# Context transposed by a DMA instead of TensorE in a two-layer gated attention and expert kernel

## The reference, cut to what matters

```python
x = x + tanh(g_xattn[0]) * decayed_sum(layernorm(x), ctx, ctx)     # q * scan(0.9 * r + ctx * ctx)
x = x + tanh(g_ffn[0]) * adapters(layernorm(x))                     # x @ W.T + one of four low-rank adapters
# attention: 16 heads of 16, sigmoid in place of softmax
k = (ctx @ Wk).reshape(b, 128, 16, 16); v = (ctx @ Wv).reshape(b, 128, 16, 16)
x = x + tanh(g_xattn[1]) * (sigmoid(mask(q @ k.T / 4)) @ v) @ Wo
x = x + tanh(g_ffn[1]) * mixture_of_8_experts_top_2(layernorm(x))
```

## Time and profile before

| | |
|---|---|
| median of three runs | 472.96 us (470.05 to 475.46) |
| the profiled execution | 474.49 us |
| its span in the trace | 472.6 us |
| PE busy | 394.9 us |
| DVE busy | 368.8 us |
| ACT busy | 331.4 us |
| POOL busy | 268.7 us |
| granted PE clock, mean | 0.969 |

### The profile page before, as it was taken

How to read it: one execution, slowest core, us unless ns; L and a number is a source line. 1 busy time by engine, 2 the same in 40 slices (tenths; PEclk the granted TensorE clock), 3 DMA queues, 4 the chain that set the end, 5 groups by cost and what they waited for, 6 DMA issues and landing times.

```text
span 472.6 us, 13099 instructions
## 1 busy us (share of the span) xinstructions
PE 394.9 (84%) x4092; PEld 308.3 (65%) x4092; DVE 368.8 (78%) x1416; ACT 331.4 (70%) x671; POOL 268.7 (57%) x313
## 2 busy tenths in 40 slices
PE   2758899998999989999899987789559999979850
PEld 1536667776776777677686765568438897967740
DVE  2888888998988889899789786367655667779994
ACT  2855788898889889898879877566706666646640
POOL 2522112545454364626545565769988888888870
PEclk9998999999999999999999999899959999999996
DMA  7245576664565555875553774624335569396985
GB/s 242 83 139 163 180 214 179 196 181 141 177 213 170 166 171 167 221 204 184 180 174 111 223 220 121 198 68 130 101 126 143 170 175 332 116 341 251 323 275 204
DMA packets 69500, 87.10 MB, mean 184 GB/s; under 512 B 9485, under 2 KB 55290, under 8 KB 69306
## 3 DMA queue, kind: packets, MB, share of 16 engines
q1 hardware_dynamic: 60074, 65.81, 46.7%
q0 software_dynamic: 6816, 18.65, 10.8%
q10 hardware_dynamic: 2544, 1.81, 1.2%
HBM read 51.07 MB, written 35.18 MB: 182 GB/s over the span
## 4 chain that ended last, share of the span: by engine, by line
PE 42%; POOL 17%; issue 14%; DVE 10%; DMA 8%; ACT 6%; ACTq 0%; POOLq 0%; DVEq 0%; SPq 0%
PE ps_J L1650 12%; PE ps_F L1650 6%; POOL store_y L771 6%; DMA store_y<-y_out,y_row 6%; PE ps_O L1764 5%; PE ps_T L1659 5%; POOL store_x L765 5%; PE ps_S L1751 5%; POOL pause_t L778 5%; PE ps_R L1689 2%; PE ps_O L1775 2%; PE ps_G L1650 2%; DMA temp_t<-in_temp 1%; DVE y_out L2934 1%; DVE xb_lo L2903 1%
## 5 line engine op out<-in xcount | busy, mean ns | idle before, releaser
L771 POOL DMA_INDIRECT store_y<-y_out,y_row x78 | 81.4, 1044 | 21.8 <-issue 16.5
L765 POOL DMA_INDIRECT store_x<-xn_E,slot_u x64 | 68.0, 1063 | 26.5 <-DVE slot_u L2633 13.6
L1089 ACT ACTIVATE prob<-ps_S 128x512 f32<-128x512 f32 x128 | 72.4, 594 | 12.7 <-PE ps_S L1751 10.0
L778 POOL TENSOR_TENSOR pause_t<-half_ones,minus_half 128x2 f32<-128x2 f32 x71 | 54.7, 770 | 1.9
L1751 PE MATMUL ps_S<-q_stack,k_stack 128*128 128x256 f16 x256 | 44.5, 276 | 5.9 <-issue 3.8
L2922 DVE TENSOR_TENSOR h_lo<-h_f,h_hi 128x512 f16<-128x512 f32 x39 | 26.9, 689 | 21.0 <-ACT h_hi L1173 9.4
L1650 PE MATMUL ps_J<-wout_hi,h_hi 128*128 x112 | 31.2, 278 | 14.3 <-DVE y_out L2934 10.9
L1764 PE MATMUL ps_O<-prob,v_wide 128*32 128x128 f32 x1024 | 41.0, 279 | 1.1 <-ACT prob L1089 0.5
L1165 ACT ACTIVATE h_f<-ps_F,bin_t 128x256 f32<-128x256 f32 x56 | 23.4, 470 | 24.5 <-PE ps_F L1650 18.9
L751 POOL TENSOR_TENSOR rstd_C<-var_C,minus_half 128x2 f32<-128x2 f32 x16 | 12.1, 759 | 40.4 <-DVE var_C L2412 40.4
L1650 PE MATMUL ps_F<-xb_hi,win_hi 128*128 128x256 f16 x112 | 31.7, 283 | 3.9 <-DVE xb_lo L2903 3.3
(11 more groups left out here) (301 smaller groups left out, 1399.5 us busy)
## 6 DMA issues: line engine op xcount, KB each, us to landing
parts_scratch<-parts SPq DMA_DIRECT2D x32, 256.0 KB
k_stack<-parts_scratch SPq DMA_DIRECT2D x64, 128.0 KB
q_stack<-parts_scratch SPq DMA_DIRECT2D x128, 64.0 KB
xb<-store_x SPq DMA_DIRECT2D x30, 257.0 KB
y_got<-store_y SPq DMA_DIRECT2D x14, 512.0 KB
c_in<-in_ctx SPq DMA_DIRECT2D x16, 256.0 KB
x_in<-in_x SPq DMA_DIRECT2D x16, 256.0 KB
store_x<-zeros SPq DMA_DIRECT2D x15, 257.0 KB, 4.6
```

Source lines behind the costliest of these rows:

```text
L765: pool.indirect_dma_start(store_x, bass.IndirectOffsetOnAxis(slot_u[q][:, at:at + 1], 0), xn_e[q][:, at, :], None).then_inc(s_scat[q], 16)
L771: pool.indirect_dma_start(store_y, bass.IndirectOffsetOnAxis(y_row[n][:, b:b + 1], 0), y_out[n][:, b, :], None).then_inc(s_y_kept[n], 16)
L778: pool.tensor_tensor(pause_t[:, :], half_ones[:, :], minus_half[:, 0:2], ALU.pow).then_inc(s_set_p, 1)
L1089: act.activation(prob[m % PROBS][:, 2 * n:2 * n + 2, :, :], bank_s[n], ACT.Sigmoid, scale=float(HD) ** -0.5).then_inc(s_prob[n], 1)
```

## The change

From pair 3 on (`PE_CTX = 3`) ctx is not transposed by PE. `hi_ctx(p)` and the new `lo_ctx(p)` split `c_in` itself, SBUF to SBUF, into `c_parts` (one buffer: in the program a part of the fp32 weights `w_f32` that is no longer needed). The new `turn_ctx(p)` on SP then issues one DMA with transpose, eight blocks of 128 x 128 fp16 (256 KB), from `c_parts` to `ct[p % 2]`, which now has two buffers. `keys(p)` and `values(p)` wait for that DMA. `hi_ctx(p)` waits until the DMA of pair p-1 has landed; `load_ctx(p)` waits for `lo_ctx(p-2)` and no longer for the transposes. Pairs 0 to 2 keep PE's transposes. The three moved steps (`hi_ctx` on ACT, `lo_ctx` on DVE, `turn_ctx` on SP) have new places in the lists; for pair 0 and 1 `hi_ctx`, and for pair 0 `lo_ctx`, stand earlier, and `transpose_ctx(1)` stands ahead of `values(0)`. Some loops at the end are written out call by call, with the same calls in the same order, and an unused helper is added.

```diff
+PE_CTX = 3
-        ct_hi = right("ct_hi", [128, KT, 256], F16)
-        ct_lo = right("ct_lo", [128, KT, 256], F16)
+        ct = [right("ct", [128, 2 * KT, 256], F16),
+              w_f32[:, 0, C_K:C_Q].bitcast(F16).rearrange("p (x c) -> p x c", x=2 * KT)]
+        c_parts = w_f32[:, 1, C_K:C_Q].bitcast(F16).rearrange("p (x c) -> p x c", x=2 * KT * 2)
...
             def load_ctx(p):
                 q = p % 2
                 need(sp, s_kv, p - 1)
-                need(sp, s_t["T"], p - 1)
+                need(sp, s_lo["T"], p - 1)
                 sp.dma_start(c_in[q][:, :, :], rows(ctx, p)).then_inc(s_c[q], 16)
+
+            def turn_ctx(p):
+                sp.wait_ge(s_lo["T"], p + 1)
+                sp.wait_ge(s_part["k"], p - 1)
+                sp.wait_ge(s_part["v"], p - 1)
+                sp.dma_start(ct[p % 2].rearrange("p x (b s) -> p (x b) s", b=2), c_parts.rearrange("p x c -> p (x c)"),
+                             transpose=True).then_inc(s_decay, 16)
...
             def hi_ctx(p):
-                need(act, s_part["k"], p)
-                need(act, s_part["v"], p)
-                hi("T", p, ct_hi[:, :, :])
+                if p < PE_CTX:
+                    need(act, s_part["k"], p)
+                    need(act, s_part["v"], p)
+                    hi("T", p, ct[0][:, 0:KT, :])
+                    return
+                if p == PE_CTX:
+                    act.wait_ge(s_wlo, 4)
+                act.wait_ge(s_c[p % 2], 16 * (p // 2 + 1))
+                act.wait_ge(s_decay, turned(p - 1))
+                act.activation(c_parts[:, 0:2 * KT, :].rearrange("p (k b) c -> p k b c", b=2),
+                               c_in[p % 2][:, :, :].rearrange("p b (k c) -> p k b c", k=KT), ACT.Copy).then_inc(s_hi["T"], 1)
...
+            def ctx_turned(p):
+                if p < PE_CTX:
+                    pe.wait_ge(s_lo["T"], p + 1)
+                else:
+                    pe.wait_ge(s_decay, turned(p))
+
+            def ctx_parts(p):
+                t = ct[0 if p < PE_CTX else p % 2]
+                return t[:, 0:KT, :], t[:, KT:2 * KT, :]
+
             def keys(last, p):
-                pe.wait_ge(s_lo["T"], p + 1)
+                ctx_turned(p)
                 bank_j_free(last, "k")
-                feature_major("k", C_K, ct_hi, ct_lo)
+                feature_major("k", C_K, *ctx_parts(p))
...
             def lo_ctx(p):
+                if p < PE_CTX:
+                    lo("T", p, ct[0][:, 0:KT, :], ct[0][:, KT:2 * KT, :])
+                    return
+                dve.wait_ge(s_hi["T"], p + 1)
+                hi_part, lo_part = (c_parts[:, 2 * KT * n:2 * KT * n + 2 * KT, :].rearrange("p (k b) c -> p k b c", b=2)
+                                    for n in range(2))
+                dve.tensor_tensor(lo_part, c_in[p % 2][:, :, :].rearrange("p b (k c) -> p k b c", k=KT), hi_part,
+                                  ALU.subtract).then_inc(s_lo["T"], 1)
...
+def turned(pair):
+    return 16 * max(1, pair - PE_CTX + 2)
...
             # PE's list, pair 11 (13 such places)
             logits(("down", 10), 7)
-            transpose_ctx(("E", 7), 11)
             project(8)
             keys(("v", 10), 11)
-            transpose_c(("T", 11), 10)
+            transpose_c(("E", 7), 10)
```

More of the change, by code:

```diff
@@ L3056, in _ @@
             down_lo(0)
-            lo("T", 1, ct_hi[:, :, :], ct_lo[:, :, :])
+            lo_ctx(1)
             statistics_b(1)
@@ L3102, in _ @@
             statistics_b(2)
-            lo("T", 2, ct_hi[:, :, :], ct_lo[:, :, :])
+            lo_ctx(3)
             means("B", 2)
@@ L3147, in _ @@
             down_lo(2)
-            lo("T", 3, ct_hi[:, :, :], ct_lo[:, :, :])
+            lo_ctx(4)
             make_x2(2)
@@ L3197, in _ @@
             variances("C", 3)
-            lo("T", 4, ct_hi[:, :, :], ct_lo[:, :, :])
             router_max(0)
@@ L3251, in _ @@
             variances("C", 4)
-            lo("T", 5, ct_hi[:, :, :], ct_lo[:, :, :])
             shifts("C", 4)
@@ L3301, in _ @@
             variances("C", 5)
-            lo("T", 6, ct_hi[:, :, :], ct_lo[:, :, :])
             copy_logits(2)
@@ L3358, in _ @@
             variances("C", 6)
-            lo("T", 7, ct_hi[:, :, :], ct_lo[:, :, :])
             shifts("C", 6)
@@ L3412, in _ @@
             router_max(4)
+            lo_ctx(9)
             router_index(4)
             shifts("C", 7)
-            lo("T", 8, ct_hi[:, :, :], ct_lo[:, :, :])
             make_x3(5)
@@ L3464, in _ @@
             rank_picked(4)
+            lo_ctx(10)
             slots(4)
-            lo("T", 9, ct_hi[:, :, :], ct_lo[:, :, :])
             shifts("C", 8)
@@ L3518, in _ @@
             variances("C", 9)
-            lo("T", 10, ct_hi[:, :, :], ct_lo[:, :, :])
             router_diff(5)
@@ L3572, in _ @@
             variances("C", 10)
-            lo("T", 11, ct_hi[:, :, :], ct_lo[:, :, :])
             means("A", 13)
@@ L3629, in _ @@
             shifts("C", 11)
-            lo("T", 12, ct_hi[:, :, :], ct_lo[:, :, :])
             shifts("B", 12)
@@ L3732, in _ @@
             variances("C", 13)
-            lo("T", 14, ct_hi[:, :, :], ct_lo[:, :, :])
             router_diff(9)
+            lo_ctx(15)
             shifts("C", 13)
@@ new lines, in _ @@
+            next(gates)
+            copy_lo(21)
+            take_rows(21)
+            hidden_lo(20)
+            add_bias(19)
+            next(gates)
+            copy_lo(22)
+            take_rows(22)
+            hidden_lo(21)
+            add_bias(20)
+            next(gates)
+            copy_lo(23)
+            take_rows(23)
+            hidden_lo(22)
+            add_bias(21)
+            next(gates)
+            copy_lo(24)
+            take_rows(24)
+            hidden_lo(23)
+            add_bias(22)
@@ new lines, in _ @@
+            next(gates)
+            copy_lo(25)
+            take_rows(25)
+            hidden_lo(24)
+            add_bias(23)
+            next(gates)
+            copy_lo(26)
+            take_rows(26)
+            hidden_lo(25)
+            add_bias(24)
+            next(gates)
+            copy_lo(27)
+            take_rows(27)
+            hidden_lo(26)
+            add_bias(25)
+            next(gates)
+            copy_lo(28)
+            take_rows(28)
+            hidden_lo(27)
+            add_bias(26)
```

726 lines of the change are left out of this document (615 added, 111 removed).

## The result

The changed kernel takes 485.54 us (median of 4, 482.79 to 490.77) against 472.40 us for the kernel before in the same rounds: 1.0255 times as long, 95% interval 1.0159 to 1.0351. The forecast was 467.0 us with a range of 461 to 481. Size and sign are both wrong.

The account below looks back on a forecast made before the run. PE was taken to lead (28.9 of 30 us busy in steady pairs), with DVE and ACT close behind. Terms -3.1, -3.3, +0.2, -0.6 and +0.8 summed to -6.0 us, giving 467.0 us, range 461 to 481.

Parts of the forecast that it names:

- The transposes off PE: PE's context transposes, 13 groups: 7, those not ahead of a waiting `project`, count as gained time, -3.1 us.
- The wait of keys for the split: PE at `keys`: waits for `ct_lo` go and those for `v_wide` shrink in part, together -3.3 us.
- ACT and DVE: Context splits fed from SBUF: ACT's slightly longer, DVE's no different, +0.2 us.
- The start: Pair 0: `lo_ctx(0)` leaves its place between the variance and `shift_B`, and `hi_ctx(0)` moves likewise, -0.6 us.
- The DMA with transpose: Queue and SP: landing in 4 to 5 us, delaying the reads of q by 0.4 us in two pairs, +0.8 us.
- the hole: SP's idle 3.8 us between the write of q and its eight reads, into which the new DMA was to fall.
- Another engine takes over: Rival, chance 0.17: DVE and ACT keep their work, PE waits for them or the reads of q; 472 us.
- Slower: Rival, chance 0.22: the DMA outlasts its hole, reads of q queue behind it, ACT may wait too; 482 to 493 us.
- The other signs: Expected in the profile: scores at pairs 4 and 10 still waiting, DVE over 27.5 of 30 us, POOL's pair 13 scatter at 304.

Follow-up runs that it names:

- h2_changed_best: The changed kernel with a third context buffer and the first three pairs in the order of the kernel before: 479.90 us, ratio 1.0178.

## Why the prediction was wrong

**The account.** From differences of ratios: the 13 DMAs 1.0% (added to before), 1.3% (taken from the changed kernel) or 1.1% (the same with three buffers), so 4.6 to 6 us. The held context buffer 0.6 to 0.7%, 3 us. What is left without both, 0.7% or 3 us, belongs to the freed slots and moved splits, where the forecast had -6.8. Three of these figures are steps from the changed kernel down to the one without either cost, so that they add up to the result is no proof; the DMAs added to the kernel before (1.0%) are the one that is independent. The single figures are good to some 0.5%, that of the changed kernel itself to 1%.

**"The transposes off PE", -3.1.** Wrong, and it is the first of the three steps that failed. The slots came off (64 transposes to 12) and the time did not. I took all slots but those ahead of a waiting `project` as time gained. A slot counts only if nothing else in the same pair makes PE wait for another engine's work, and I looked for such a wait only behind the slot itself. In the pair of runs that differ by these slots and the source of the splits, their 5.3 us came back as 3.1 us more idle in front of `project` and 2.1 in front of the transposes of `xn_C`. In the changed kernel the wait for `av` grew from 3.5 to 4.9 us, just under the 5 that I had named as a sign, and that for `xn_C` from 1.9 to 6.0, which the text didn't name.

**"The wait of keys for the split", -3.3.** The second step that failed. The groups of the first matmuls of `keys`, odd and even pairs, 60 to 275 us, beside the earlier trace rows:

```profile
L1932 PE MATMUL ps_J<-w_f,w_hi 128*128 128x256 f16 x56 | 9.5, 272 | 1.0 <-ACT v_wide L1293 1.0
...
L1932 PE MATMUL ps_J<-ct,w_hi 128*128 128x256 f16 x48 | 8.2, 273 | 1.6 <-ACT v_wide L1293 1.0 <-DMA ct<-w_f 0.6
```

The weight loads of the same matmuls, in the kernel before and in the changed one:

```profile
L1650 PEld LDWEIGHTS ps_J<-ct_hi,w_hi 128*128 128x128 f16 x52 | 5.1, 97 | 5.9 <-DVE ct_lo L2456 5.1 <-issue 0.2
```

```profile
L1932 PEld LDWEIGHTS ps_J<-w_f,w_hi 128*128 128x128 f16 x56 | 5.3, 98 | 2.9 <-issue 1.8
...
L1932 PEld LDWEIGHTS ps_J<-ct,w_hi 128*128 128x128 f16 x48 | 4.5, 98 | 2.8 <-issue 1.1 <-DMA ct<-w_f 1.0
```

No split is waited for; one pair waits for the DMA. But the idle time did not go, it changed its name: 2.6 us in front of the matmuls against 2.3, and 5.7 in front of the loads against 5.9. The waits for `v_wide`, of which I took 1.3 us off, stayed: 2.0 us against 1.7. The text had reckoned with the wait that ended last, and not with the one that stood next behind it.

**ACT and DVE, +0.2.** ACT's split takes 625 ns from SBUF, as estimated, DVE's 684, as before. But "reads two operands either way, and I take no difference" missed that with the second operand in SBUF instead of PSUM it is POOL that becomes slower. In the changed kernel `rstd_C` has a mean of 801 ns against 739, from 60 to 275 us, 0.8 us in 13 calls, and ACT's wait for `shift_C` rises from 1.3 to 4.3 us; so the stretching can be at most 0.8 of these 3.0 us, and where the rest comes from was not tried. The Trainium skill states it (GPSIMD Engine Reference, "Key points"): the engine shares its SBUF interfaces with VectorE, with contention against DVE instructions that have two SBUF inputs. The trace agrees, with 0.69 to 1.06 us for one call; I had not weighed that sentence.

**The start, -0.6.** Wrong. `shift_B` comes at 15.69 us, not earlier, and DVE's row shows why (before: the earlier trace rows):

```profile
15.69 0.16 DVE L2855 SCALAR_TENSOR_TENSOR shift_B<-mv_B,rstd_B 128x2 f32<-128x2 f32 x1 [0.67 <-POOL rstd_B L833]
```

It waits for POOL. The split had filled a gap. The loss of 3.9 us at pair 0 comes from a wait that the prediction did not list at all.

**The DMA with transpose, +0.8.** Its sizes held: 2.05 to 2.25 us of 16 engines (bounds 0.9 and 2.3, so the high one, from queue 10's time per packet), a median landing of 4.9 us in the run that adds it to before, 3.1 to 5.6 in the changed kernel. SP's issue is 1.2 to 2.0 us, not 0.4, and the run with one block, where it is 1.1, shows no cost that can be told from none. What failed, the third step, is the price: 0.4 us in two pairs, 0.8 in all, where the runs have 4.6 to 6 us and the scores wait for reads in 6 places (5 in the changed kernel). I let it cost only "where it outlasts the hole" ahead of the reads of q, and it cost at less than half the 5.3 us of queue time from which I had reckoned. Whether the hole shelters a part of it is not settled, since the run that moved the DMAs brought in a wait of its own. Which of the other transfers on the queue it delays, the reads of k or the writes of q and k, wasn't tried either. The Trainium skill's two sentences that I had weighed (Advanced Engine Details and Errata, "X-Bar Transpose (TRN2)": as fast as plain DMAs; VectorE: DVE Perf Modes, "The three transpose paths": 1309 ns a block) do not fit here: it takes 2.4 times the engine time of a plain copy of the same bytes, and eight blocks land in 3.1 to 5.6 us, not in the 10.5 that I had estimated from the figure for one.

**The rivals.** *Another engine takes over* is what happened to the gain; its 472 us is some 3 us under the changed kernel with both costs taken off (1.0067). *Slower* had the sign, but not its reason: it let the DMA cost from 5.3 us of queue time on, and it costs at 2.25. Its second part, ACT standing in front of a split for the landing, is there once, with 1.4 us. The loss of the held buffer was in no rival: I had read `need(sp, s_lo["T"], p - 1)` in the diff and compared only the place of the loads, not what is queued on SP behind one that waits. So this cost, 3 us, is a term that the sum did not have.

**The sum's range.** "With the bounds of the terms it is 465 to 470" does not follow. The bounds given for the terms (0 and -5.7, -2.3 and -5.1, +0.2, 0 and -0.7, and for the DMA 0 or its +0.8) add up to 461.7 to 471.7 us. The result lies outside these too.

**The other signs.** Scores at pairs 4 and 10 still wait, and so do 6, 11, 13 and 15. DVE is at 26.9 of 30, not over 27.5, since PE did not get faster. POOL's first scatter of pair 13:

```profile
318.73 1.04 POOL L847 DMA_INDIRECT store_x<-xn_E,slot_u  x1 [4.50 <-DVE slot_u L3080]
```

It is at 318.7 instead of the 304 forecast and the 310.1 of the earlier trace rows; the rest of the program is 1 us longer than before.

No version of the change is faster than before. The best that computes the reference is `h2_changed_best` at 1.0178.

## What to carry to other kernels

When a step gets its input from another place, ask when the old place comes free and what is queued behind the load that waits for it: here that wait was worth 3 us, and 8 in the old order, and it stood in one line of the diff. Do not price a DMA on a busy queue (a share of 0.61 over the pairs here) by the one hole that it is put in, and get its packets from the nearest kind: 1056 are not the 144 of a copy. Behind a wait that you take away, look for the one that stands next: in front of `keys` the idle time stayed. And before a slot on the fullest engine is counted as gained, take it out in a run and see what else that run changes: here the first such run was 2.4% slower, by the held buffer, and only with a third buffer did it show that the slots bring nothing.

## What the runs showed of the hardware that wasn't expected

A DMA with transpose of eight 128x128 fp16 blocks inside SBUF has 1056 packets and takes 2.05 (changed kernel) to 2.25 us (added to before) of all 16 engines, a copy of the same 256 KB 144 packets and 0.92 us. SP's issue takes 1.09 to 1.20 us with one block and 1.23 to 2.0 with eight, against 0.47 for most of the copies. A POOL operation of 0.69 us on 128x2 elements takes 0.98 to 1.23 us when it begins at most 0.3 us behind a DVE operation of 0.69 us that reads two operands from SBUF: in all eight calls of the kernel without PE's transposes and with three buffers that began during such an operation, it ended 0.54 to 0.59 us behind the end of that operation, whenever it had begun. It takes 0.69 to 0.72 us beside the same split when one operand is in PSUM (79.12 and 128.90 us of the kernel before).

Two things stay open: whether POOL's 2.4 us are the whole reason why the kernel without PE's transposes is 0.3% (all reads of q) and 0.7% (half) slower than its like with them, of which only the second is clear of noise, and why SP needs 5.5 us for the reads of pair 15 when the pairs start earlier.
